# A six-stage decoder layer pair on one core: first-block weights of the recurrent stage loaded and prepared during the feed-forward; one activation table set for the logarithm and exponential of every norm

## The reference, cut to what matters

```python
x = x + linear_attention(_layernorm(x), ...)        # "la"
x = x + cross_attention(_layernorm(x), ctx, ...)    # "x0"
x = x + ternary_ffn(_layernorm(x), ...)             # "ffn"
x = x + four_recurrent_blocks(_layernorm(x), ...)   # "ma"
x = x + cross_attention(ctx, _layernorm(x), ...)    # "x1"
x = x + top_2_experts(_layernorm(x), ...)           # "moe"

def _layernorm(x, axis=-1, eps=1e-05):
    m = mean(x); v = var(x)
    return (x - m) / sqrt(v + eps)

# one of the 4 recurrent blocks; i picks its weights
h = layer_norm(x, norm_w[i], norm_b[i])
u, z = split(h @ in_w[i]);  u = silu(conv4(u, cw[i]) + cb[i])
dbl = u @ xw[i];  dt = softplus(dbl[:64] @ dtw[i] + dtb[i])
A = -exp(A_log[i]);  y = selective_scan(u, dt, A, B, C, D[i])
x = x + (y * silu(z)) @ ow[i]
```

## Time and profile before

| | before |
|---|---|
| median of 3 runs | 1915.6 us |
| the profiled execution | 1913.99 us, span 1912.2 us |
| busy: PE, DVE, ACT, POOL | 1336.5, 1442.0, 1111.3, 1141.0 us |

### The profile page before, as it was taken

One profiled execution on the slowest core, in us unless ns is written; L12 is line 12 of the kernel. 1 busy time (PEld: TensorE's weight loads), 2 busy tenths in 40 slices (PEclk: granted clock), 3 DMA queues, 4 the chain that ended last, 5 costly groups with the idle time before them and its releaser, 6 DMA issues. The chain is left out here.

```text
span 1912.2 us, 23467 instructions
## 1 busy us (share of the span) xinstructions
PE 1336.5 (70%) x6930; PEld 664.4 (35%) x6931; DVE 1442.0 (75%) x2464; ACT 1111.3 (58%) x2443; POOL 1141.0 (60%) x742
## 2 busy tenths in 40 slices
PE   3777798985565566656555656565436899999868
PEld 2555465553221122212111211121103566666523
DVE  3554688977329999999999999999992766666634
ACT  2443787875545656665556566655534777777720
POOL 2101465640049999999999999999970443343400
PEclk8899899995676777787777777877668899999978
DMA  3000000000134323242334313323303000000000
GB/s 104 1 2 2 1 2 1 1 1 1 23 155 178 155 117 125 114 178 114 152 155 177 152 69 137 155 114 151 155 0 89 1 1 1 2 1 1 1 0 22
DMA packets 51983, 134.53 MB, mean 70 GB/s; under 512 B 19076, under 2 KB 28568, under 8 KB 39448
## 3 DMA queue, kind: packets, MB, share of 16 engines
q1 hardware_dynamic: 49112, 130.78, 18.2%
q10 hardware_dynamic: 2496, 2.36, 0.4%
q0 software_dynamic: 256, 0.01, 0.0%
HBM read 114.26 MB, written 18.87 MB: 70 GB/s over the span
## 5 line engine op out<-in xcount | busy, mean ns | idle before, releaser
L1498 POOL TENSOR_TENSOR ma_hs<-ma_dtuR,ma_Bt 128x1024 f32<-128x1024 f32 x256 | 596.9, 2359 | 20.4 <-PE ps L1574 12.9
L1657 ACT ACTIVATE ps<-ma_dtR,ma_A 128x512 f32<-128x512 f32 x512 | 332.6, 681 | 345.6 <-DVE ma_hs L1791 286.7
L820 POOL TENSOR_TENSOR x_pr<-x_pr,x_rec 128x512 f32<-128x512 f32 x256 | 267.8, 1046 | 341.6 <-DVE x_rec L1062 341.6
L1785 DVE TENSOR_TENSOR_SCAN ps<-ps,ma_hs 128x1024 f32<-128x1024 f32 x176 | 401.7, 2282 | 0.0
L1574 PE MATMUL ps<-ma_hs,ma_fold 128*32 128x512 f32 x1024 | 179.1, 835 | 206.2 <-POOL ma_hs L1506 174.1
L1028 ACT ACTIVATE x_pr<-x_sm,x_mx 128x256 f32<-128x256 f32 x512 | 255.1, 501 | 52.3 <-DVE x_mx L1053 48.5
L1791 DVE TENSOR_TENSOR ma_hs<-ps,ma_Ct 128x1024 f32<-128x1024 f32 x176 | 215.4, 1224 | 6.1
L1541 PE MATMUL ps<-ma_hn,ma_w_tap 128*128 128x512 f32 (+3 forms) x256 | 144.8, 719 | 96.0 <-ACT ma_hn L1675 84.2
L1785 DVE TENSOR_TENSOR_SCAN ma_hs<-ps,ma_hs 128x1024 f32<-128x1024 f32 x80 | 182.5, 2281 | 34.1 <-ACT ps L1657 32.2
L1506 POOL TENSOR_TENSOR ma_hs<-ma_hs,ma_Ct 128x1024 f32<-128x1024 f32 x80 | 188.4, 2355 | 22.9 <-DVE ma_hs L1785 22.9
L885 PE MATMUL ps<-ident,x_pr 128*128 128x128 f32 x1024 | 160.5, 283 | 5.2 <-DVE x_pT L958 4.6
(11 more groups left out here) (308 smaller groups left out, 2224.6 us busy)
## 6 DMA issues: line engine op xcount, KB each, us to landing
ma_dtuR<-ma_dtu_d SPq DMA_DIRECT2D x32, 1024.0 KB, 6.7
ma_dtR<-ma_dt_d SPq DMA_DIRECT2D x32, 1024.0 KB, 8.6
ma_Bt<-ma_bc_d SPq DMA_DIRECT2D x16, 1024.0 KB, 5.0
ma_Ct<-ma_bc_d SPq DMA_DIRECT2D x16, 1024.0 KB, 6.9
ma_dtu_d<-ma_dtu SPq DMA_DIRECT2D x32, 256.0 KB, 2.0
ma_dt_d<-ma_dt SPq DMA_DIRECT2D x32, 256.0 KB, 2.3
ma_cwb<-in_L_attn_conv_w_dram SPq DMA_DIRECT2D x4, 512.0 KB
x_m<-in_mask_BxSxS_fk_dram SPq DMA_DIRECT2D x1, 2048.0 KB, 11.8
```

The lines of the kernel that those rows point to most:

```text
L820: pool.tensor_tensor(pr[:, r, :, :], pr[:, r, :, :], rec[:, r, :].unsqueeze(2).broadcast_to([P, 2, L]), ALU.mult).then_inc(pr_done, 1)
L1498: pool.tensor_tensor(hs[:, k % SLOTS, :, :], dtuR[:, unit(f, h), q, :].unsqueeze(1).broadcast_to([P, 2, CH]), rows(Bt, k), ALU.mult).then_ ...
L1657: e = act.activation(c.ps[:, 2 * (k % 2) + a, :], dtR[:, unit(f, h), q, :], ACT.Exp, scale=A[:, (f // QUARTERS) % 2, h, q, no:no + 1])
L1785: dve.tensor_tensor_scan(out, pair(k), slot(k), 0.0, ALU.mult, ALU.add).then_inc(scan_done, 1)
```

## The change

Each norm asks for the set that has both functions ahead of its squares, and ACT does Ln and Exp of one chunk before it goes to the next. The tiles and semaphores of the recurrent weights move into a class `RecurrentWeights`, made at the start of the kernel; its `load` and `prepare` for block 0 are called on SP and POOL in the ffn's block. The order of the DMAs within `load` changes (w_in and cwb first). The part of `weights` that needs ACT's exponential stays in the recurrent stage as `rates`.

```diff
@@ load_stage; the same in Norm.on_scalar and norm_stage
+                act.preload_act_table_set("natural_log_exp_and_others")
...
                 for h in range(4):
                     act.wait_ge(var_done, h + 1)
                     act.activation(lnv[:, h * CH:(h + 1) * CH], c.ps[:, h, :], ACT.Ln, bias=c.eps[:, 0:1]).then_inc(lnv_done, 1)
-                for h in range(4):
                     act.wait_ge(lnv_done, h + 1)
                     act.activation(rstd[:, h * CH:(h + 1) * CH], lnv[:, h * CH:(h + 1) * CH], ACT.Exp,
                                    scale=-0.5).then_inc(rstd_done, 1)
@@ ffn_stage
         with nc.Block() as block:
+            @block.sync
+            def _(sp):
+                c.weights.load(sp, g, 0)
+
+            @block.gpsimd
+            def _(pool):
+                c.weights.prepare(pool, c, 0)
@@ class RecurrentWeights
+    def prepare(self, pool, c, i):
+        b, gq = i % 2, 4
+        pool.wait_ge(self.weights_in, self.LOADS * (i + 1))
+        for h in range(2):
+            pool.tensor_copy(self.w_gate[:, b, h, :].rearrange("p (q e) -> p q e", q=gq),
+                             self.w_in[:, DI + h * P:DI + (h + 1) * P].rearrange("p (e q) -> p q e", q=gq)).then_inc(self.tap_w, 1)
+        pool.tensor_tensor(self.w_tap[:, b, :, :], self.w_in[:, 0:DI].unsqueeze(1).broadcast_to([P, TAPS, DI]),
+                           self.cwb[:, :, :].rearrange("p c t -> p t c"), ALU.mult).then_inc(self.tap_w, 1)
+        for h in range(2):
+            pool.tensor_scalar(self.dD[:, b, h, :].rearrange("p (q e) -> p q e", q=gq),
+                               c.ident[:, :].rearrange("p (e q) -> p q e", q=gq),
+                               self.vec[:, b, 4 + h:5 + h], None, ALU.mult).then_inc(self.dd_done, 1)
@@ mamba_stage
-                load(0)
                 for f in range(-1, NF - 1):
...
-                weights(0)
+                rates(0)
                 dt_times_u(0)
```

More of the change, by code:

```diff
@@ L1116, in _, with ffn_stage @@
                 finish(B)
-def ffn_stage(c):
+def ffn_stage(c, g):
     nc = c.nc
@@ L1328, in mamba_stage @@
     with Stage(c, "ma") as s:
[L1329 to L1338, removed]
+        w = c.weights
+        w_gate, w_tap, w_x, w_dt, w_out, dD, A, vec = w.w_gate, w.w_tap, w.w_x, w.w_dt, w.w_out, w.dD, w.A, w.vec
+        weights_in, tap_w, dd_done = w.weights_in, w.tap_w, w.dd_done
         fold = s.sb("fold", [P, E32])
@@ L1355, in mamba_stage @@
         dtu_d = nc.dram_tensor("ma_dtu_d", [2, 2, P, CH], F32, kind="Internal").ap()
-        names = ("weights_in consts tap_w dd_done a_exp a_done centred squared var_done lnv_done rstd_done scaled "
+        names = ("consts a_exp a_done centred squared var_done lnv_done rstd_done scaled "
                  "hn_done u_ps u_done z_ps z_done x_ps xp_done dt_ps abs_done exp_done ln_done dt_done dtu_done first_set "
@@ L1365, in mamba_stage @@
         dt_out, dt_in, dtu_in = (dt_out0, dt_out1), (dt_in0, dt_in1), (dtu_in0, dtu_in1)
-        LOADS = 21 * 16
+        LOADS = w.LOADS
         PA, PB, Y = 6, 7, (4, 5)
@@ L1434, in _ @@
                     if f >= 0 and f % QUARTERS == 1 and f // QUARTERS + 1 < NBLK:
-                        load(f // QUARTERS + 1)
+                        i = f // QUARTERS + 1
+                        if i >= 2:
+                            sp.wait_ge(resid, QUARTERS * (i - 1))
+                        w.load(sp, g, i)
                     sp.wait_ge(xp_done, F + 1)
@@ L1471, in _, with rates @@
                                    base=NI - 1, pattern=[[NI, E32]], channel_multiplier=-1).then_inc(consts, 1)
[L1473 to L1486, removed]
+                def rates(i):
                     pool.wait_ge(a_exp, i + 1)
-                    pool.tensor_scalar(A[:, b, :, :, :], A[:, b, :, :, :], -1.0, -1.0e-20, ALU.mult, ALU.min).then_inc(a_done, 1)
+                    pool.tensor_scalar(A[:, i % 2, :, :, :], A[:, i % 2, :, :, :], -1.0, -1.0e-20, ALU.mult, ALU.min).then_inc(a_done, 1)
                 def times_b(k):
@@ L1520, in _ @@
                     if f % QUARTERS == 2 and f // QUARTERS + 1 < NBLK:
-                        weights(f // QUARTERS + 1)
+                        w.prepare(pool, c, f // QUARTERS + 1)
+                        rates(f // QUARTERS + 1)
                     for t in range(ITEMS):
@@ L2022, in decoder_kernel @@
             constants(c)
+            c.weights = RecurrentWeights(c)
             c.ctx = layer0
@@ L2040, in decoder_kernel @@
             cross_attention_stage(c, "x0", P // NH, False, (c.wqk[:, 2, :], c.wqk[:, 3, :], c.wvo[:, 2, :], c.wvo[:, 3, :]))
-            ffn_stage(c)
+            ffn_stage(c, g)
         norm_stage(c, "n4", c.xT, c.xn)
```

42 lines of the change are left out of this document (41 added, 1 removed).

## The result

The changed kernel takes 1894.62 us (median of 4 runs, 1893.11 to 1898.23). In the same comparison the kernel before takes 1916.3 us (4 runs, 1914.8 to 1919.82). The ratio is 0.9887, with an interval from 0.9867 to 0.9907. That is 21.7 us less, by the medians, where 18.6 were forecast. The profiled execution happened to be the longest of the four, 1898.23 us with a span of 1896.5; the forecast for it was 1895.4.

A forecast was written before the change was run, and what follows sets the result against it. Outside the scans, one chain from engine to engine between stages was taken to bound the kernel. 8.7 + 1.1 + 2.4 + 8.7 - 2.3 = 18.6 us less, from 1915.6 to 1897.0 us; range 1891.5 to 1901.0.

The forecast's parts named there:

- Weights: Recurrent stage's start: loading and preparing weights during the ffn removes the wait, so the tap projection starts 8.7 us earlier.
- Norms: Seven norms: 2.17 us less in load stage, x0, ffn, n4; 0.5 in moe and x1; 2.44 in n5.
- The choice that Ln overlaps with the Exp ahead of it: ACT in the norms: the next Ln follows 0.51 us after an Exp's start; without overlap 0.14 more per chunk.
- The added load: Each norm's start: the 1.28 us table load ahead of the squares is hidden, cost taken 0.
- The collision: In the ffn, POOL's weight preparation holds up DVE's four tiny operations: 2.3 us lost, bounds 0 and 3.1.
- the first meeting: In the ffn, DVE's first tiny operation waits for the end of POOL's `w_tap` product, 1.69 us late.
- part of the second: In the ffn, DVE's later tiny operations may meet POOL's two `dD` scalings; part of that wait was counted.
- Two rivals: ACT in the norms: hidden drain per load, 1886 us, chance 0.01; costly function changes inside a set, 1951 us, chance 0.02.
- The slower one: Norms: each function change inside one set costs time, deciding from 0.44 us; 1951 us at a whole load each; chance 0.02.
- The clock: PE's granted clock across stages: no term in the forecast sum, considered only as a rival.
- the forecast's clock rival: PE's clock stays high after shorter pauses in ffn, x0, x1, moe, 1 to 2 us each; 1894 us; chance 0.10.

The follow-up runs named there:

- e1: The kernel before with only the norms' part (preload and turns in all seven norms), weights still loaded in the recurrent stage: 1901.18 us, ratio 0.9922.
- e2: The changed kernel with the norms as before, so only the weights loaded and prepared in the ffn: 1906.09 us, ratio 0.995.
- e4: The changed kernel with POOL's weight preparation moved from the ffn to n4, DMAs staying in the ffn: 1891.21 us, ratio 0.9866.
- e7: e4 with ACT's order in every norm skewed (Ln 0, Exp 0, Ln 1, Ln 2, Exp 1, Ln 3, Exp 2, Exp 3): 1887.94 us.
- e3: The changed kernel with the preload kept, but four Ln and then four Exp instead of turns: 1899.02 us, ratio 0.9911.
- e5: The changed kernel with two more table loads between squares and first Ln in all seven norms: 1910.51 us, ratio 0.996.
- e10: e2's kernel, unchanged, profiled once more: 1898.45 us.
- e6: The changed kernel without the preloads of the common table set, turns kept: 1936.09 us, ratio 1.0106.
- e8: The kernel before, unchanged, profiled once more: 1916.84 us.

## Why the prediction was right, and where it was off

**Weights: right in place and size.** 8.60 us of 8.7, and next in line were the norm's chain and the affine, as said. e1 puts the 16.60 us back and e2 keeps the 7.97. That figure holds with PE's first two matmuls as slow as in the kernel before (2.05 us for both); in e4 and e7, where they take 1.10, it is 7.15.

**Norms: right.** The load stage (-2.14) and n5 (-2.44) read as forecast; ffn and n4 do too where POOL and the clock don't disturb them (e1: 75.34 and 12.38 us, -2.19 and -2.14 against the two stages of before). The choice that Ln overlaps with the Exp ahead of it, for which there was no row, holds: 0.54 us from start to start where the bounds were 0.51 and 0.65. The added load is hidden as forecast: two squares stand together behind it, and the third follows at PE's pace. In moe, too, DVE ends 6.64 us after the last square's start instead of 7.15, in the same profile in which moe as a whole is only 0.3 us shorter.

**The collision: right in mechanism, too large by 0.6 us.** 2.3 us was the term. Measured from the first of the four small operations to L1270, it is 2.37 us (429.67 to 432.04) where it was 0.69 in the kernel before: 1.68, and 1.88 in the second profile. POOL started 12.83 us after the stage's first matmul (12.93 forecast) and the small operation stood at 14.80 (14.82), so the first meeting was nearly as drawn: 1.46 us longer, where I had 1.69. The prediction read the earlier trace rows as "the second finishes late by what was left of the first". The rows say less: 0.34 us were left and 0.20 were lost, 0.43 left and 0.28 lost. The 16-column operation lost 1.46 of 1.59.

The term that was mis-sized is the second one, "part of the second", for which I had 0.6 us and which came to 0.22. POOL's two scalings `dD`, shown above as one row, are two instructions; this is the first:

```profile
431.25 0.73 POOL L1360 TENSOR_SCALAR ma_dD<-ident,ma_vec 128x128 f32<-128x128 f32 x1
```

It ends at 431.98, and L1266, the last of the small operations, ends at 432.01. In all six profiles in which these small operations overlap a scaling L1266 ends 0.03 us behind the end of one (e2's at 439.11, its second scaling at 439.08; both profiles of the changed kernel, e3, e5 and e10 the same). Without POOL the last of the four ends 0.49 us after the first does; here it ends 0.71 us after it, just behind the scaling, so that 0.22 us was all that was left to lose. L1265, 0.12 us longer than before, ends 0.22 us ahead of the scaling; why it does isn't shown. The Trainium skill ("SBUF — State Buffer", on the shared port pair) has the later of the two wait for the other's whole instruction; the trace agrees for the product, at whose end (431.26 against 431.30) the 16-column operation finished, and for L1266 beside the scaling.

**No hidden price of a load or of a change of function.** Two rivals rested on it. The slower one (0.44 us per change and more) falls with the 0.71 and 0.54 us between starts in the norms, which leave no room for it. The Trainium skill ("ScalarE: Activation LUTs", What ACT_TABLE_LOAD costs) counts 2.66 us for a switch of sets. e5 and e6 speak against it: 14 loads on the path cost 15.9 us, and 32 on the path cost 41.5 us, both by the medians. An estimate by the page's price for the 14 loads of e5 is 37 us.

**The clock: the term that I set to zero.** The terms at their measured size make 4 x 2.14 + 2 x 0.5 + 2.4 + 8.6 - 1.7 = 18.9 us. The medians give 21.7, two pairs of profiles 15.8 (1913.99 to 1898.23) and 23.7 (1916.84 to 1893.17). Most of what lies between shows as PE's granted clock, in rows of both signs, and the forecast's clock rival had only the one sign. The first 10 us of x0, busy time by stretch of the kernel before and after:

```profile
185.50:195.50 10.00, 10.00 (x16) 4.01 (x16) 0.00 (x0) 5.03 (x8) 2.69 (x4) 0.69 0.01 2
```
```profile
183.60:193.60 10.00, 8.49 (x16) 3.48 (x16) 1.57 (x3) 7.57 (x12) 2.72 (x4) 0.86 0.00 1
```

The same 16 matmuls run at 0.69 and then at 0.86. This needn't be the change's doing: the kernel before shows 0.85 there in its second profile, and e4, whose program is the changed one's up to the ffn, 0.70. x0 as a whole is 231.3 to 232.1 us long in the changed kernel twice, e1, e3 and e7, 234.49 in e4, and 235.80 and 235.15 in the kernel before, so how much of its 4.5 us beyond the norm's 2.14 comes from the change stays open.

In x1 the granted clock of the first 10 us falls, from 0.85 (the kernel before) to 0.72 (changed). PE's eight centring matmuls take 6.42 us instead of 5.21: the first 1.2 us of the 2.4 that x1 grew, in place of 0.5 less. This part goes with the shorter n5. It is there in all profiles with n5 at 14 us (the changed kernel twice, e1, e4, e6, e7), and in e5, whose n5 is 16.34 us, they take 5.25. Another 1.3 us are lost right behind x1's norm, in its first sixteen projection matmuls (L845, under other numbers in the experiments). PE's timeline in the kernel before, the changed kernel, e5 and e7, in this order:

```profile
1467.33 5.41 PE L845 MATMUL ps<-xn,x_wq 128*128 128x256 f32 x16 [3.81 <-DVE xn L345]
```
```profile
1450.14 6.68 PE L845 MATMUL ps<-xn,x_wq 128*128 128x256 f32 x16 [3.30 <-DVE xn L345]
```
```profile
1465.05 6.63 PE L851 MATMUL ps<-xn,x_wq 128*128 128x256 f32 x16 [5.64 <-DVE xn L349]
```
```profile
1446.12 5.26 PE L867 MATMUL ps<-xn,x_wq 128*128 128x256 f32 x16 [2.96 <-DVE xn L358]
```

The sixteen take 6.68 us in all five profiles with the plain turns and the short n5, and 5.41 in all five with the old order. The loss is in e5 too and not in e7, so it goes with the plain turns of x1's own norm and not with n5; the granted clock of the 20 us from x1's 10th on is 0.91 in the kernel before, 0.83 in the changed kernel and in e5, and 0.90 in e7. The pause ahead of these matmuls (3.81, 3.30, 5.64, 2.96 us) doesn't order them, and what the order of the norm does to them isn't shown. Both parts less the norm's 0.5 make 2.0 of the 2.4 us. All profiles with turned norms and the plain order have the longer x1 (368.03 to 368.46 us in the changed kernel twice, e1, e4 and e6, 369.42 in e5 with two loads more), none with the old order has it (365.8 to 366.1 us, before, e2, e3, e8, e10), and e7 is at 364.99.

The first attention's 1.8 us and the 1.6 us ahead of the load stage need no change of the program: e2 and e10, one kernel, have 138.79 and 136.88 us for the one, 20.75 and 22.12 for the other. The forecast was 2.4 us too high. The gain is 3.1 us larger than forecast: 0.3 by the terms at their measured size, the rest by clock and the spread of the medians; that of before is 1916.3 in this comparison, 0.7 above the one I started from. That the median came so near is in part luck, since moe's level alone moves an execution by 5 us and the sum has no term for it.

What stays open: what sets the level in moe's 40th to 50th us, in x0 and in x1's two places. No run here changed PE's activity on purpose.

## What to carry to other kernels

Where Ln and Exp of a short norm stand between two engines that wait, first put both functions into one table set, loaded while ACT waits anyway, and only then take them in turns: turns without the set were slower than no change, and the set without turns brought 1.64 of the load stage's 2.14 us. An order in which no Exp but the first stands right behind its Ln brought another 0.35 us per norm. Check the stage behind as well: what turns gained in n5, PE lost again in x1. When weights are prepared early on GpSimd, choose a stretch where VectorE works from PSUM or not at all, since here even a 128x16 SBUF operation stood behind a long GpSimd product. Compare stage by stage over more than one execution before a rest of some us is explained: the changed kernel's last stage differed by 5 us between two profiles.

## What the runs showed of the hardware that was not expected

- A load of a set that is already active still takes 1.28 us: n5, x1 and moe each have one, ahead of their squares, though in the kernel before the norms there did Ln and Exp without any load, so that a set with both was active.
- The 128x16 operation with scalars (L1262) waits like a wide one: 1.63 us instead of 0.17 beside GpSimd's 2.85 us product. The reciprocal behind it lost nothing beside a 128x128 scaling of 0.73 us, and the last small operation ended 0.03 us after a scaling's end in six profiles; in the changed kernel only 0.22 us were left to lose by then.
- Two ACT operations without a dependence start 0.51 to 0.58 us apart at 128x512, a dependent one 0.71 to 0.72 after its source, so a dependence costs ACT 0.13 to 0.21 us per pair; e7 shortens the row of eight by 0.44 us by order alone.
- A shorter pause of PE didn't always come with a higher clock. Ahead of x1, 6.89 us without a matmul went with 0.72 granted in the changed kernel (twice) and in e7, and 9.32 us with 0.85 and 0.84 in the kernel before and in e2. In e5, 9.24 us went with 0.84.
